# Two GNN layers on one core: x transposed in fp32 and halved on leaving PSUM, counts leaving PSUM two banks at a time, block copies shared by two engines, products two tiles late

## The chip, the core and the metric

One core of a Trainium2 chip runs the whole program. The metric is the device time of one execution in microseconds (us); lower is better. The engines are TensorE (PE in profiles), VectorE (DVE), ScalarE (ACT), GpSimd (POOL) and SyncE (SP), which issues the transfers.

## What is computed

3125 nodes with 256 features and 50,000 edges (src, dst), sorted by dst. Two graph layers, each followed by a residual sum and a layer norm:

```python
def _L0_gnn_ref(features, rows, cols, W0, b0, W1, b1):      # rows = src, cols = dst
    ...
    neigh = segment_sum(vals[:, None] * x[cols], rows)      # vals = 1 / degree
    cat = jnp.concatenate([x, neigh], axis=1)
    return relu(cat @ W.T + b)                              # twice, with W0 and W1

def _L1_gnn_ref(feat, W_self, W_neigh, src, dst):
    h_sparse = _maxk(feat @ W_neigh, 32)
    neigh = segment_sum(h_sparse[src], dst) / maximum(deg, 1)
    return feat @ W_self + neigh

x = _layernorm(x + _L0_gnn_ref(...))
x = _layernorm(x + _L1_gnn_ref(...))
```

## The kernel before

Sums over edges are made as products with a matrix of counts: C[s, d] is the number of edges between node s and node d. It is held in SBUF as 25 x 25 blocks of 125 x 125 counts in f16 (`ct`), and in HBM (`c_dram`) for the last layer. The program has four parts: the edges are sorted into windows (to about 58 us); the counts are built tile by tile ("the build", about 58 to 233 us, the part that the change touches); the first GNN's two sums and products; the second GNN.

**The build.** Tile t of 25 goes through these steps, each a program of its engine in a fixed written order, tied to the others by semaphores:

- VectorE writes one-hot rows for the edges of each window (`quick_hots(t, k)`, L790): 25 windows of a tile, in 3 sets. The rows of tile t+1 are written while tile t is counted; a set's buffer is free when its windows are counted.
- TensorE counts: `fill(t, f)` (L1336) multiplies the one-hot rows of 4 windows into one of 4 PSUM banks, 7 fills a tile.
- ScalarE copies each bank into a row of blocks in SBUF, `slab` (`quick_copy`, L1062), and SyncE stores the slab to `c_dram`.
- TensorE turns the slab's 25 blocks of the tile before in 4 groups (`transposes(t-1, par, g)`, L1359) into two banks, which alternate.
- VectorE copies each group from PSUM into `ct` (`tr_copy`, L796).

Beside this, the first product of x with W0 is made one tile of rows at a time. Values are carried as two f16 halves, a high and a low one, so that three f16 products stand for one fp32 product. GpSimd makes scale, high half and low half of x (`split_x`: L479, L480, L483), TensorE turns the four f16 quarters (`own_transposes`, L1373), ScalarE copies them to `x_t16` (`own_t`, L1073), TensorE multiplies (`own_product(t, 0)` and `(t, 1)`, L1367, three 512-column matmuls each), ScalarE copies the result to `own` (`own_copy`, L1080), and GpSimd splits its second half into `xs` (`split_a0`: L504, L506). The rows of x lie in `xs` as fp32 until then.

Ahead of the first products GpSimd also scales and splits the four weight matrices into halves (`split`, L479 to L483): 3 operations for each half of W0 and of W1, and 3 each for the two of the last layer. Its order is x tile 0, W0, x tile 1, W1, the last layer's two, and then, for each tile, the split of x and of the result. `own_copy(t)` waits for `split_a0(t-2)`, which frees its buffer.

The program's branch on the edges' total (`If`) holds the build's loop; the last tile's turns, and its product, stand behind the branch.

## Time and profile before

| | us |
|---|---|
| median of 3 runs (lowest, highest) | 754.15 (753.65, 754.87) |
| the profiled execution | 752.71 |
| its span, first to last instruction | 750.9 |
| TensorE busy in the span | 640.3 (85%) |
| VectorE busy | 542.4 (72%) |
| GpSimd busy | 370.4 (49%) |
| ScalarE busy | 318.6 (42%) |

The span is the profiled execution less what lies around the first and the last instruction (1.8 us). Shares of the whole span mix parts with different limits: what counts here is the build, in which VectorE has no idle time once it runs evenly, and the waits at its start.

### The profile page before, as it was taken

Reading aid. Unit: us, or ns where it says so; the run is one execution under the profiler, and the core shown is the slowest. Engines: PE = TensorE matmul, PEld = TensorE weight load, DVE = VectorE, ACT = ScalarE, POOL = GpSimd, SP = SyncE. Lnnn points to the kernel's source line nnn. Section 1 sums busy time; section 2 is a strip of 40 time slices with the busy share of each in tenths; the row PEclk is TensorE's granted clock in tenths of the full one; section 3 lists DMA queues with packets and bytes.
Section 4 is the critical chain, followed back from the end, with each engine's and each line's share of the span. In section 5 each row is a group of like instructions: output and inputs, shape, how many; then the busy total and the mean of one; then the engine's idle time right before and its main releaser. Section 6 shows DMA issues by size and latency. Waiting matters only on the chain.

```text
span 750.9 us, 11604 instructions
## 1 busy us (share of the span) xinstructions
PE 640.3 (85%) x4048; PEld 346.2 (46%) x4049; DVE 542.4 (72%) x1210; ACT 318.6 (42%) x672; POOL 370.4 (49%) x379
## 2 busy tenths in 40 slices
PE   2635387888778399999999999999999979999996
PEld 2524276666654144444444444444444434444443
DVE  6685489999981888888888546877877772844343
ACT  2122377777771567676776523333333320100000
POOL 2008999999984888888888222233233210000000
PEclk9755789999998699999999999999999999999999
DMA  9300346555553010111101046556555513320000
GB/s 229 48 20 22 99 128 213 149 150 149 147 157 96 9 42 29 41 33 38 41 29 42 23 137 180 157 171 180 168 159 178 173 57 103 111 82 21 28 21 28
DMA packets 39832, 72.99 MB, mean 97 GB/s; under 512 B 3609, under 2 KB 32496, under 8 KB 39770
## 3 DMA queue, kind: packets, MB, share of 16 engines
q1 hardware_dynamic: 39770, 72.20, 33.2%
q8 instruction: 35, 0.57, 0.3%
q14 instruction: 27, 0.22, 0.1%
HBM read 38.81 MB, written 33.38 MB: 96 GB/s over the span
## 4 chain that ended last, share of the span: by engine, by line
PE 53%; DVE 30%; POOL 5%; DMA 5%; issue 3%; ACT 2%; SPq 1%; DVEq 0%; POOLq 0%; ACTq 0%
PE bank L1461 26%; PE bank L1549 17%; DVE hots L790 12%; PE bank L1367 8%; DVE ct L796 5%; DMA xs<-in_x_dram 3%; DVE tree L872 2%; DVE tree L871 2%; POOL w_parts L483 1%; POOL w_scaled L479 1%; PE bank L1373 1%; DMA own_in<-own_dram 1%; POOL w_parts L480 1%; DVE xmax L633 1%; DMA bias_sb<-in_L_gnn_b_dram 1%
## 5 line engine op out<-in xcount | busy, mean ns | idle before, releaser
L1461 PE MATMUL bank<-xs,ct 125*128 125x512 f16 x625 | 147.2, 387 | 0.0
L1461 PE MATMUL bank<-a,ct 125*128 125x512 f16 x625 | 142.8, 379 | 0.0
L1549 PE MATMUL bank<-xs,ct 125*128 125x512 f16 x625 | 135.7, 379 | 0.0
L1062 ACT ACTIVATE slab<-bank 125x500 f16<-125x500 f32 (+1 forms) x175 | 92.5, 566 | 53.9 <-PE bank L1336 47.7
L790 DVE TENSOR_TENSOR hots<-iota,jobs 128x2048 f16<-128x2048 f16 (+1 forms) x75 | 107.4, 1434 | 2.7 <-issue 1.5
L1549 PEld LDWEIGHTS bank<-xs,ct 125*128 125x128 f16 x625 | 62.1, 99 | 72.3
L1461 PEld LDWEIGHTS bank<-xs,ct 125*128 125x128 f16 x625 | 61.9, 101 | 70.5 <-issue 4.9
L1461 PEld LDWEIGHTS bank<-a,ct 125*128 125x128 f16 x625 | 61.0, 99 | 68.2
L1161 ACT ACTIVATE a<-ct 125x1000 f16<-125x1000 f16 (+1 forms) x75 | 80.2, 1069 | 9.5 <-POOL tr_sb L548 8.6
L1359 PE MATMUL bank<-ident,slab 125*128 125x125 f16 x625 | 53.3, 224 | 30.8 <-DVE ct L796 25.9
L1367 PE MATMUL bank<-w_lay,tr_sb 128*128 128x512 f16 x300 | 73.0, 379 | 4.8 <-ACT tr_sb L1137 4.8
L562 POOL TENSOR_TENSOR part<-t,part 125x256 f16<-125x256 f32 x25 | 16.8, 672 | 117.1 <-ACT part L1201 117.1
L796 DVE COPY ct<-bank 125x882 f16<-125x882 f16 (+1 forms) x100 | 53.8, 556 | 25.2 <-PE bank L1359 25.2
L1336 PE MATMUL bank<-hots 128*128 128x125 f16 x625 | 54.3, 227 | 4.7 <-DVE hots L790 4.1
L887 DVE SCALAR_TENSOR_TENSOR t<-bank,rdeg,own_in 125x256 f32<-125x256 f32 x50 | 24.2, 484 | 46.9 <-PE bank L1461 42.3
L1359 PEld LDWEIGHTS bank<-ident,slab 125*128 125x128 f16 x625 | 39.2, 101 | 40.9 <-issue 22.9
L1223 ACT ACTIVATE sd<-mv,epsb 125x1 f32<-125x1 f32 x25 | 7.4, 294 | 113.9 <-DVE mv L992 113.9
L988 DVE SCALAR_TENSOR_TENSOR a<-bank,rdeg_dst,a 125x256 f32<-125x256 f32 x25 | 12.1, 482 | 56.5 <-PE bank L1549 56.4
L534 POOL TENSOR_TENSOR own_in<-own_in,bias_sb 125x256 f32<-125x256 f32 x50 | 39.3, 786 | 25.1 <-DMA own_in<-own_dram 25.1
L1336 PEld LDWEIGHTS bank<-hots 128*128 128x128 f16 x625 | 43.7, 103 | 15.1 <-DVE hots L790 4.5
L479 POOL TENSOR_TENSOR xscaled<-xs,scales 125x256 f32<-125x256 f32 x25 | 35.0, 1398 | 31.2 <-DVE scales L770 31.1
L1137 ACT ACTIVATE tr_sb<-bank 128x500 f16<-128x500 f32 x50 | 29.1, 582 | 47.2 <-PE bank L1373 47.2
(182 smaller groups left out, 1009.5 us busy)
## 6 DMA issues: line engine op xcount, KB each, us to landing
c_dram<-slab SPq DMA_DIRECT2D x25, 683.6 KB
ct<-c_dram SPq DMA_DIRECT2D x25, 683.6 KB
own_in<-own_dram SPq DMA_DIRECT2D x50, 125.0 KB
own_dram<-own SPq DMA_DIRECT2D x25, 125.0 KB
own_dram<-own_st SPq DMA_DIRECT2D x25, 125.0 KB
x_in<-in_x_dram SPq DMA_DIRECT2D x25, 125.0 KB
z_dram<-z_st SPq DMA_DIRECT2D x25, 125.0 KB
a<-z_dram SPq DMA_DIRECT2D x5, 625.0 KB
```

Source lines behind the costliest of these rows:

```text
L479: nc.gpsimd.tensor_tensor(scaled, given, by, ALU.mult).then_inc(pool_step, 1)
L534: nc.gpsimd.tensor_tensor(own_in[k % 2][:, :], own_in[k % 2][:, :], bias_sb[:, :], ALU.add).then_inc(own_biased, 1)
L790: v.tensor_tensor(hots[k][:, :, :, :].rearrange("p w g (a d) -> p (w g) a d", d=2), iota, job, ALU.is_equal).then_inc(win_hot, 1)
L796: v.tensor_copy(ct[:, TG0[g]:TG0[g] + TG[g], t, :], tr16[g % 2][0:P, 0:TG[g], 0:PC]).then_inc(tr_free, 1)
L1062: a.activation(slab3[t % 2][:, :, f * BW * QW:(f * BW + n) * QW].rearrange("p b (w d) -> p b w d", d=QW), bank[(FILLS * t + f) % 4][0:P, 0 ...
L1137: a.activation(tr_sb[i % 2][:, :, 0:P], tp[i % 2], ACT.Copy).then_inc(tp_copied, 1)
L1161: a.activation(unread[:, 0:(hi - lo) * P].rearrange("p (b s) -> p b s", s=P), ct[:, lo:hi, T, 0:P], ACT.Copy, accum_out=deg_part[:, T, k:k ...
L1336: last = mm(bank[n % 4][:, at:at + QKEY], hot[:, 0, :], hot[:, 1, 0:QKEY], start=True, stop=True, skip_group_check=True)
L1359: last = nc.tensor.transpose(tr16[g % 2][:, i, 0:P], slab[par][:, (TG0[g] + i) * P:(TG0[g] + i) * P + 128], ident16[:, 0:P])
L1367: last = mm(out, lhs(2 * pt + h), w[:, h, q, :], start=h == 0 and k == 0, stop=h == 1 and k == 2, skip_group_check=True)
L1461: ins = mm(agg[k % 3][0:lhs.shape[1], :], lhs, parts[l][:, t, :], start=t == 0, stop=t == NT - 1, skip_group_check=True)
L1549: ins = mm(out3[T % 8][0:lhs.shape[1], :], lhs, xs[:, b, :], start=b == 0, stop=b == NT - 1, skip_group_check=True)
```

## The change

- One-hot sets and fills become the same four groups, of 7, 6, 6 and 6 windows. A fill writes a pair of banks (two pairs in all), and one ScalarE copy empties a pair: 4 copies a tile instead of 7.
- The slab's blocks are turned in groups of 5, 8, 5 and 7. ScalarE copies groups 0 and 2 out of one bank, VectorE groups 1 and 3 out of the other.
- x is no longer split by GpSimd. TensorE turns its fp32 rows (two 128-column blocks), ScalarE writes the scaled high half (`own_t`), and VectorE the low half (`own_low`), both from PSUM. `own_product` waits for the low half.
- W0's high halves are written by ScalarE after tile 1, its low halves by VectorE (`w0_low`) at iteration 2.
- The products start in iteration 2 (tile of rows 0), iteration 3 has two (1 and 2), and from iteration 4 on each has one (t-1) as before.
- Some small work ahead of the build: two maxima of x instead of three and one over them, fewer steps for the scales, the clearing of two banks before the bounds instead of after them.

The core of the diff (the branch for other edge totals, semaphores and names of buffers are left out):

```diff
-SETS = [(0, 8), (8, 16), (16, 25)]
-BW = 4
-FILLS = 7
+SETS = [(0, 7), (7, 13), (13, 19), (19, 25)]
+FILLS = len(SETS)
 SHIFTS = [64, 32, 16, 8]
-XC = [0, 9, 17, 25]
+XC = [0, 13, 25]
+OWN = {2: [0], 3: [1, 2], **{t: [t - 1] for t in range(4, NT)}}
...
-TG = [7, 6, 6, 6]
-TG0 = [0, 7, 13, 19]
+TG = [5, 8, 5, 7]
+TG0 = [0, 5, 13, 18]
...
-            def split_x(t):
-                if t > 1:
-                    pool.wait_ge(own_tp, t - 1)
-                split(xparts[t % 2][:, 0:F], xparts[t % 2][:, F:2 * F], xscaled[:, :], xs32[:, t, :],
-                      scales[0:P, 0:1].broadcast_to([P, F]), x_split, t + 1)
...
-            split_x(0)
-            split_w(w_t[0], w0_parts, 3, w0_split, 1)
-            split_x(1)
             split_w(w_t[1], w_parts[0], 4, w_split, 1)
...
-            for t in range(2, NT):
-                split_x(t)
-                split_a0(t - 2)
-            split_a0(NT - 2)
-            split_a0(NT - 1)
+            for t in range(NT):
+                split_a0(t)
...
-            for c in range(3):
-                v.tensor_reduce(xmax[:, c:c + 1], xs32[:, XC[c]:XC[c + 1], :].rearrange("p t f -> p (t f)"), X, ALU.max,
+            for c in range(2):
+                v.tensor_reduce(stat[0:P, c:c + 1], xs32[:, XC[c]:XC[c + 1], :].rearrange("p t f -> p (t f)"), X, ALU.max,
...
+            def w0_low(h):
+
+                dve.wait_ge(w0_hi, h + 1)
+                lo = w0_parts[:, h, 1, :].rearrange("p (a f) -> p a f", a=2)
+                hi = w0_parts[:, h, 0, :].rearrange("p (a f) -> p a f", a=2)
+                v.scalar_tensor_tensor(lo, w_t[0][:, h::2, :], scales[:, 3:4], hi, ALU.mult, ALU.subtract).then_inc(w0_split, 1)
+
+            def own_low(t):
+
+                dve.wait_ge(own_tcopied, t + 1)
+                v.scalar_tensor_tensor(x_t16[:, 2:4, 0:P], xp, scales[:, 0:1], x_t16[:, 0:2, 0:P], ALU.mult, ALU.subtract
+                                       ).then_inc(own_tlo, 1)
...
-                    tr_copy(t - 1, 0)
-                    if t + 1 < NT:
+                    if t == 2:
+                        w0_low(0)
+                        w0_low(1)
+                    tr_copy(t - 1, 1)
+                    more = t + 1 < NT
+                    if more:
                         quick_hots(t + 1, 0)
-                    tr_copy(t - 1, 1)
-                    if t + 1 < NT:
+                    own = OWN.get(t, [])
+                    if more:
                         quick_hots(t + 1, 1)
-                    tr_copy(t - 1, 2)
+                    for o in own[:1]:
+                        own_low(o)
                     tr_copy(t - 1, 3)
-                    if t + 1 < NT:
+                    if more:
                         quick_hots(t + 1, 2)
-                for g in range(4):
+                        quick_hots(t + 1, 3)
+                    for o in own[1:]:
+                        own_low(o)
+                for g in (1, 3):
...
-                n = min(BW, NT - BW * f)
-                a.activation(slab3[t % 2][:, :, f * BW * QW:(f * BW + n) * QW].rearrange("p b (w d) -> p b w d", d=QW),
-                             bank[(FILLS * t + f) % 4][0:P, 0:n * QKEY].rearrange("p (w b d) -> p b w d", b=NT, d=QW),
+                lo, hi = SETS[f]
+                n = hi - lo
+                a.activation(slab3[t % 2][:, :, lo * QW:hi * QW].rearrange("p b (w d) -> p w b d", d=QW),
+                             pair[f % 2][0:P, 0:n, 0:QKEY].rearrange("p w (b d) -> p w b d", d=QW),
                              ACT.Copy).then_inc(slab_ready if f == FILLS - 1 else win_read, 1)
...
-                a.activation(x_t16[:, :, 0:P], tp[2], ACT.Copy).then_inc(own_tcopied, 1)
+                a.activation(x_t16[:, 0:2, 0:P], xp, ACT.Copy, scale=scales[:, 0:1]).then_inc(own_tcopied, 1)
...
+                for h in range(2):
+                    a.activation(w0_parts[:, h, 0, :].rearrange("p (a f) -> p a f", a=2), w_t[0][:, h::2, :], ACT.Copy,
+                                 scale=scales[:, 3:4]).then_inc(w0_hi, 1)
...
                     for f in range(FILLS):
                         quick_copy(t, f)
-                        if f == 1:
-                            own_t(t - 1)
-                    own_copy(t - 1, (t - 1) % 2, (t - 1) // 2)
+                        if f == 0:
+                            tr_copy(t - 1, 0)
+                        if f == 1 and own:
+                            own_t(own[0])
+                        if f == 2:
+                            tr_copy(t - 1, 2)
+                    if t == 1:
+                        ready_for_own()
+                    for i, o in enumerate(own):
+                        if i:
+                            own_t(o)
+                        own_copy(o, o % 2, o // 2)
+                for g in (0, 2):
+                    tr_copy(NT - 1, g)
...
-                k = 0 if f < 2 else 1 if f < 4 else 2
-                pe.wait_ge(win_hot, 3 * t + k + 1)
-                if n >= 4:
-                    t4, f4 = divmod(n - 4, FILLS)
-                    if f4 == FILLS - 1:
-                        pe.wait_ge(slab_ready, t4 + 1)
+                pe.wait_ge(win_hot, n + 1)
+                if n >= 2:
+                    t2, f2 = divmod(n - 2, FILLS)
+                    if f2 == FILLS - 1:
+                        pe.wait_ge(slab_ready, t2 + 1)
                     else:
-                        pe.wait_ge(win_read, (FILLS - 1) * t4 + f4 + 1)
-                for u in range(BW * f, min(BW * f + BW, NT)):
-                    hot, at = hots[k][:, u - SETS[k][0]], u % BW * QKEY
-                    last = mm(bank[n % 4][:, at:at + QKEY], hot[:, 0, :], hot[:, 1, 0:QKEY], start=True, stop=True,
+                        pe.wait_ge(win_read, (FILLS - 1) * t2 + f2 + 1)
+                for u in range(SETS[f][1] - SETS[f][0]):
+                    last = mm(pair[f % 2][:, u, 0:QKEY], hots[f][:, u, 0, :], hots[f][:, u, 1, 0:QKEY], start=True, stop=True,
                               skip_group_check=True)
...
-            def own_transposes(t, par):
-
-                pe.wait_ge(x_split, t + 1)
-                turn(tp[2], xparts[par], own_tp)
+            def own_transposes(t, rows_):
+
+                for h in range(2):
+                    last = nc.tensor.transpose(xp[:, h, :], rows_[:, h * 128:(h + 1) * 128], identx[:, :])
+                last.then_inc(own_tp, 1)
...
                 if h == 0:
-                    pe.wait_ge(own_tcopied, t + 1)
+                    pe.wait_ge(own_tlo, t + 1)
                     pe.wait_ge(own_copied, t + 1)
...
                 for t in range(1, NT):
                     par = (t - 1) % 2
+                    own = OWN.get(t, [])
                     fill(t, 0)
                     transposes(t - 1, par, 0)
+                    for o in own[:1]:
+                        own_transposes(o, xs32[:, o, :])
+                    transposes(t - 1, par, 1)
                     fill(t, 1)
-                    own_transposes(t - 1, par)
-                    transposes(t - 1, par, 1)
                     fill(t, 2)
+                    transposes(t - 1, par, 2)
+                    for o in own[:1]:
+                        own_product(o, 0)
+                    transposes(t - 1, par, 3)
                     fill(t, 3)
-                    transposes(t - 1, par, 2)
-                    own_product(t - 1, 0)
-                    fill(t, 4)
-                    fill(t, 5)
-                    transposes(t - 1, par, 3)
-                    own_product(t - 1, 1)
-                    fill(t, 6)
+                    for o in own[:1]:
+                        own_product(o, 1)
+                    for o in own[1:]:
+                        own_transposes(o, xs32[:, o, :])
+                        own_product(o, 0)
+                        own_product(o, 1)```

What this does to the order on the engines, in an iteration of the build's loop away from its ends.

TensorE before, iteration 4: `hots` rows are counts, `slab` rows turned blocks, `xparts` rows x turned in f16, `w_parts` rows the product's halves.

```order
L1336 MATMUL bank<-hots_63 128x125 x3
L1373 MATMUL bank<-ident_51,xparts_85 128x125 [waits x_split]
L1373 MATMUL bank<-ident_51,xparts_85 128x125 x3
L1359 MATMUL bank<-ident_51,slab_61 128x125 [waits tr_free,slab_ready]
L1359 MATMUL bank<-ident_51,slab_61 128x125 x5
L1336 MATMUL bank<-hots_64 128x125 [waits win_read,win_hot]
```

TensorE in the changed kernel, the same stretch and on to the product's second half (`xs` rows turn x in fp32):

```order
L1374 MATMUL pair<-hots_63 128x125 x6
L1397 MATMUL bank<-ident_51,slab_61 128x125 [waits tr_free0,slab_ready]
L1397 MATMUL bank<-ident_51,slab_61 128x125 x4
L1417 MATMUL bank<-identx,xs 128x125 x2
L1397 MATMUL bank<-ident_51,slab_61 128x125 [waits tr_free1,slab_ready]
L1397 MATMUL bank<-ident_51,slab_61 128x125 x7
...
L1405 MATMUL bank<-w_parts,x_t_84 125x512 [waits w0_split,own_copied,own_tlo]
L1405 MATMUL bank<-w_parts,x_t_84 125x512 x2
L1397 MATMUL bank<-ident_51,slab_61 128x125 [waits tr_free1,slab_ready]
L1397 MATMUL bank<-ident_51,slab_61 128x125 x6
L1374 MATMUL pair<-hots_66 128x125 [waits win_read,win_hot]
```

The turn of x no longer waits for GpSimd, and the product's first half, which waits for the low half (`own_tlo`), stands ahead of the last group of turned blocks.

VectorE before, one iteration:

```order
L796 COPY ct<-bank 125x7x126 [waits tr_done]
L790 TENSOR_TENSOR hots_63<-iota_67,jobs 128x2048 [waits win_done]
L796 COPY ct<-bank 125x6x126 [waits tr_done]
L790 TENSOR_TENSOR hots_64<-iota_67,jobs 128x2048 [waits win_done]
L796 COPY ct<-bank 125x6x126 [waits tr_done] x2
L790 TENSOR_TENSOR hots_65<-iota_67,jobs 128x2304 [waits win_done]
```

VectorE in the changed kernel, one iteration:

```order
L797 COPY ct<-bank 125x8x126 [waits tr_done]
L791 TENSOR_TENSOR hots_63<-iota_68,jobs 128x1792 [waits win_done]
L791 TENSOR_TENSOR hots_64<-iota_68,jobs 128x1536 [waits win_done]
L779 SCALAR_TENSOR_TENSOR x_t_84<-bank,scales,x_t_84 128x2x125 [waits own_tcopied]
L797 COPY ct<-bank 125x7x126 [waits tr_done]
L791 TENSOR_TENSOR hots_65<-iota_68,jobs 128x1536 [waits win_done]
L791 TENSOR_TENSOR hots_66<-iota_68,jobs 128x1536 [waits win_done]
```

Two of four block copies are gone, a fourth one-hot operation and the low half of x have come; the low half stands directly ahead of the copy of the last group of turned blocks.

## Rows read from the trace of the kernel before

**Rows 1.** The page: busy time by engine in the span.

```profile
PE 640.3 (85%) x4048; PEld 346.2 (46%) x4049; DVE 542.4 (72%) x1210; ACT 318.6 (42%) x672; POOL 370.4 (49%) x379
```

**Rows 2.** Windows of the even build: stretch, busy (instructions), PEclk, DMA share, GB/s.

```profile
102.30:216.39 114.09, 90.37 (x1143) 71.71 (x1141) 114.09 (x134) 85.67 (x171) 109.86 (x96) 1.00 0.55 163
```

**Rows 3.** Chain of waits in an even iteration: start, us, what.

```profile
144.42 1.62 DVE hots L790
...
148.30 0.53 DVE ct L796
148.83 1.13 DVE hots L790
```

**Rows 4.** Groups by form, even build: count, busy, mean ns, idle before.

```profile
L1062 ACT ACTIVATE slab<-bank 125x500 f16<-125x500 f32 x114 | 64.7, 607 | 21.4 <-PE bank L1336 21.2
L1080 ACT ACTIVATE own<-bank,unscale 125x512 f32<-125x512 f32 x19 | 12.8, 675 | 0.0
L1062 ACT ACTIVATE slab<-bank 125x125 f16<-125x125 f32 x19 | 6.0, 317 | 6.4 <-PE bank L1336 6.4
```

**Rows 5.** Timeline of TensorE, even iteration: start, us, instruction [idle before].

```profile
148.97 0.49 PE L1359 MATMUL bank<-ident,slab 125*128 125x125 f16 x6 [0.56 <-DVE ct L796]
149.30 0.81 PE L1367 MATMUL bank<-w_parts,x_t 128*125 128x512 f16 x3
149.95 0.60 PE L1336 MATMUL bank<-hots 128*128 128x125 f16 x8
```

**Rows 6.** Timeline of GpSimd, the same stretch.

```profile
142.89 1.32 POOL L504 CAST xs<-own 125x256 f16<-125x256 f32 x1
144.29 0.67 POOL L506 TENSOR_TENSOR xs<-own,xs 125x256 f16<-125x256 f32 x1
```

**Rows 7.** Timeline of VectorE, to the fourth iteration: start, us, instruction [idle before].

```profile
60.06 1.35 DVE L790 TENSOR_TENSOR hots<-iota,jobs 128x2304 f16<-128x2304 f16 x1
...
73.57 0.55 DVE L796 COPY ct<-bank 125x756 f16<-125x756 f16 x1 [7.06 <-PE bank L1359]
...
94.05 0.55 DVE L796 COPY ct<-bank 125x756 f16<-125x756 f16 x1 [9.81 <-PE bank L1359]
...
100.18 0.60 DVE L796 COPY ct<-bank 125x882 f16<-125x882 f16 x1
```

**Rows 8.** Timeline of GpSimd: its first operation, weights beside VectorE and in quiet.

```profile
58.94 0.61 POOL L479 TENSOR_TENSOR xscaled<-xs,scales 125x256 f32<-125x256 f32 x1 [31.08 <-DVE scales L770]
...
76.98 1.90 POOL L479 TENSOR_TENSOR w_scaled<-w_t,scales 128x512 f32<-128x512 f32 x1
...
87.45 1.04 POOL L479 TENSOR_TENSOR w_scaled<-wn_nat,scales 128x512 f32<-128x512 f32 x1
```

**Rows 9.** The page: a VectorE operation that reads PSUM in fp32.

```profile
L887 DVE SCALAR_TENSOR_TENSOR t<-bank,rdeg,own_in 125x256 f32<-125x256 f32 x50 | 24.2, 484 | 46.9 <-PE bank L1461 42.3
```

**Rows 10.** Timeline of TensorE: fp32 turns, and a product at half clock.

```profile
30.09 1.15 PE L1240 MATMUL bank<-identf,w_nat 128*128 128x128 f32 x8 [0.96 <-ACT w_t L1025]
...
95.28 1.49 PE L1367 MATMUL bank<-w_parts,x_t 128*125 128x512 f16 x3
```

**Rows 11.** Windows of TensorE: stretch, busy, PEclk, DMA share, GB/s.

```profile
94.00:96.00 2.00, 2.00 (x17) 0.50 0.00 0
222.00:226.00 4.00, 1.99 (x26) 1.00 0.43 129
226.00:230.00 4.00, 1.54 (x22) 0.69 0.50 140
```

**Rows 12.** Timeline of TensorE at the end of the build.

```profile
223.44 0.22 PE L1336 MATMUL bank<-hots 128*128 128x125 f16 x1
225.66 0.55 PE L1359 MATMUL bank<-ident,slab 125*128 125x125 f16 x7 [2.01 <-issue]
...
230.46 2.77 PE L1367 MATMUL bank<-w_parts,x_t 128*125 128x512 f16 x6
```

**Rows 13.** Timeline of VectorE, the last copy of the build.

```profile
230.71 0.55 DVE L796 COPY ct<-bank 125x756 f16<-125x756 f16 x1 [2.61 <-PE bank L1359]
```

More of the change, by code:

```diff
@@ L543, in sum_tree @@
                 nc.gpsimd.tensor_tensor(tree[:, :], tree[:, :], quint[4], ALU.add).then_inc(tree_ready, 1)
-            pool.wait_ge(tr_free, 4 * NT + 2)
+            for done in tr_free:
+                pool.wait_ge(done, 2 * NT + 1)
             sum_tree(0)
@@ L816, in _ @@
             with dve.If(total > E - 1):
-                for k in range(3):
+                for k in range(FILLS):
                     quick_hots(0, k)
@@ L844, in _ @@
                 scales_out()
-                with dve.Fori(0, NW) as w:
-                    general_hots(w)
-            dve.wait_ge(tr_free, 4 * NT + 2)
+                for u in range(WT):
+                    general_hots(u)
+                for h in range(2):
+                    w0_low(h)
+                with dve.Fori(1, NT) as t:
+                    for u in range(WT):
+                        general_hots(t * WT + u)
+                        if u == 1:
+                            v.tensor_copy(xstage[:, :], xs32[:, ds(t - 1, 1), :].rearrange("p o f -> p (o f)")).then_inc(own_staged, 1)
+                        if u == 2:
+                            own_low(t - 1)
+            own_low(NT - 1)
+            for free in tr_free:
+                dve.wait_ge(free, 2 * NT + 1)
             dve.wait_ge(slab_stored[0], BOTH * 13)
@@ L1001, in _ @@
             act.sem_inc(win_free, 2)
-            act.sem_inc(tr_free, 2)
+            for free in tr_free:
+                act.sem_inc(free, 1)
             act.wait_ge(firsts_b, 2)
@@ L1163, in _ @@
             act.wait_ge(tr_zeroed, 2)
-            act.wait_ge(tr_free, 4 * NT + 2)
+            for free in tr_free:
+                act.wait_ge(free, 2 * NT + 1)
             for k in range(len(DG)):
```

98 lines of the change are left out of this document (53 added, 45 removed).

## Prediction

> **What bounds the kernel now.** The page comes first: TensorE is busy 85% of the span, VectorE 72% [rows 1], but the change is in the build alone, so I read that part by windows and by its chain of waits. From 102.30 us, where the build runs evenly, to 216.39 us pass 19 iterations of 6.005 us, and VectorE is busy for all of it; TensorE has 90.4 of 114.1 us, ScalarE 85.7, GpSimd 109.9 [rows 2]. The chain there is VectorE alone: one-hots, the first of 1.62 and the last of 1.13 us, and block copies, such as one of 0.53 us [rows 3]. Both one-hots have 2048 elements, and the first is 0.49 us longer. GpSimd's L506 is running when it starts (144.29 us for 0.67 us), and L504 takes 1.32 us, most of it beside a one-hot [rows 6]. So an iteration loses half a us where the two share something.
>
> Ahead of the even part VectorE waits 7.06 and 9.81 us for turned blocks [rows 7]. TensorE stands there behind products and turns of x whose halves GpSimd has yet to write. That is the second thing the change touches.
>
> **What the change does, step by step.** I count from start to start of operations, and call the sets H0 to H3, the groups of turned blocks T0 to T3, the counts F0 to F3, the turn of x X, the product's halves P0 and P1, VectorE's copies R1 and R3, and the low half of x L.
>
> *VectorE's own work.* The quiet one-hot takes 1.13 us for 2048 elements, the copy 0.53 for 882 [rows 3]: 0.515 ns an element and 0.075 us fixed, if both run alike. So H0 (1792) is 1.00 us and H1 to H3 (1536) 0.865 each: 3.6 us. The copy of 882 elements takes 0.53 us [rows 3]; R1 has 1008 (0.6) and R3 882 (0.53). L reads 250 fp32 elements a partition from PSUM; the nearest row, of that kind with 256, takes 0.484 us [rows 9]. The sum, with L overlapped as usual (0.4), is 5.1 us against 6.0. By this alone an iteration would win 0.9 us.
>
> *But VectorE does not run alone.* The order is L, R3 on VectorE and P0, T3 on TensorE: P0 waits for L, T3 stands behind P0, and R3 waits for T3. Between L and R3 VectorE has nothing to do. TensorE's three 512-column matmuls take 0.65 us (149.30 to 149.95), six turned blocks 0.33 us (148.97 to 149.30), 0.055 each, and the last of a group ends 0.16 us later [rows 5]. From L's start to R3's: 0.48 (L) + 0.14 (to TensorE, as from the copy's end at 148.83 to the blocks' start at 148.97 [rows 3, 5]) + 0.65 (P0) + 0.39 (T3, 7 blocks) + 0.20 (end and signal) = 1.86 us. The circle through VectorE is then 1.86 + 0.53 (R3) + 1.73 (H2, H3) + 0.60 (R1) + 1.87 (H0, H1) = 6.6 us.
>
> *A second circle, through TensorE, is as long.* R1 waits for T1, which is late: 0.62 (L) + 0.65 (P0) + 0.39 (T3) + 0.33 (F3) + 0.65 (P1) + 0.39 (F0) + 0.28 (T0) + 0.28 (X) + 0.44 (T1) + 0.20 + 0.60 (R1) + 1.87 (H0, H1) = 6.7 us. X is two fp32 turns: eight took 1.15 us at full clock, 0.14 each [rows 10]. ScalarE's circle is shorter. Its copy costs 0.317 us for 125 columns and 0.607 us for 500 [rows 4], 0.77 ns a column; back to back four copies of a pair (0.80 and three of 0.70), two of 630 elements (0.59 each), the high half (0.3) and the result (0.57) give 5.0 us. The new write pattern (runs of five elements) has no row: bounds are nothing and a fifth more, 0.6 us, still under the circle.
>
> *The collision stays.* L504 starts when the result is copied, by this schedule 3.8 us after L's start, while H3 runs (3.3 to 4.2); it ends behind it, and L506 runs from about 4.5 to 5.2, over H0's start at 4.8. H0 loses 0.45 us, as the first one-hot does now. Both circles hold H0, so the period is 7.1 us. Without the collision it would be 6.6. **I take 7.1**, for the row shows this very pair [rows 3, 6]. On what the two share, the Trainium skill (SBUF — State Buffer, Who interferes with whom) says that VectorE and GpSimd have one pair of ports, held by one of them for a whole instruction. The trace agrees, with 1.62 against 1.13 us; were it not so here, the period would be 6.6 us.
>
> *The start.* Before, the fourth iteration's first copy starts at 100.18 us [rows 7]. Now GpSimd no longer stands between TensorE and x or W0. VectorE ended the last one-hot of tile 1 at 60.06 + 1.35 = 61.4 us [rows 7]; that set is smaller now, which gives 61.0, and I count the dropped small steps at nothing. Iteration 1 costs 4.7 us of VectorE's own, about 1 for waiting on T3 at half clock, and 1 for collisions with the weights' split, which goes on: to 67.7. The two `w0_low` (512 fp32 elements from two SBUF sources) add 1.2 and up to 0.9 of waiting: to 69.8. R1, H0, H1 and 0.8 of collisions: L at 73.1. From there 7.1 us to the next L, and 2.2 more since TensorE has been idle and begins at half clock, where three matmuls read 1.49 instead of 0.81 us [rows 5, 10] and the granted clock 0.50 [rows 11]: L of iteration 3 at 82.4. That iteration has a second product: X, L, 1.3 us for both halves, all ahead of F0: 7.1 + 3.4 = 10.5 us to the next L, at 92.9. Its iteration began 2.9 us earlier (R1, H0 with its collision, H1), at 90.0. **The start wins 10.2 us** (bounds 5 and 15: a little more half clock, or none and no collisions).
>
> GpSimd must have split the result of tile 0 when ScalarE wants to write that of tile 2, at about 88 us. It has 12 weight operations, of 1.04 us in quiet and 1.90 beside VectorE, from about 58.9 us on [rows 8]: with each at 1.9 they are done at 82, and `split_a0(0)` at 84. Covered.
>
> *The even part.* 20 iterations from there: 20 x (7.1 - 6.005) = +21.9 us. The last one has no one-hots; from its first copy to the end of the last count are 2.8 us, before 3.4: -0.6.
>
> *The tail.* Before, the last count ends at 223.66 us, the last turns follow a 2.01 us gap behind the branch, and the product starts at 230.46 us [rows 12], a quarter us before VectorE's last copy starts at 230.71 [rows 13]. Now that product waits for the last L, which stands behind that copy and behind VectorE's own branch. If leaving it costs VectorE what it costs TensorE, 2 us, L starts 2.6 us after the copy does and the product ends 3 us later than before: +3 (bounds 0.5 and 3.5).
>
> The sum: -10.2 + 21.9 - 0.6 + 3.0 = +14.1 us on the profiled execution's 752.7, that is 766.8; the median of the runs shown is 1.4 us above that execution: 768.
>
> **The rivals.**
>
> *No collision* (0.20). L504 and L506 fall between one-hots: the period is 6.65, the even part +12.9, the sum +5.1, 759 us. Against it: they follow the result's copy at a fixed distance. For it: 0.3 us of shift would free H0.
>
> *VectorE's own work sets the pace* (0.12, the faster side). TensorE has P0 and T3 done before VectorE wants R3, because L's data are there early or the last blocks wait elsewhere. Then the period is 5.1 plus a collision, 5.6: 20 x -0.4 = -8.1, the sum -10.2 - 8.1 - 0.6 + 3 = -16, 738 us. It decides from a period of 6.4 on, where 20 x 0.39 equals what start and tail leave over. For it: VectorE is now the pace alone [rows 2, 3]. Against it: the written order of L, P0, T3, R3.
>
> *The sum is nothing* (0.05): a period of 6.4, or of 6.6 with the whole 15 us won at the start and a short tail: 754 us.
>
> *TensorE's clock falls in every iteration* (0.08). It would be idle some 2 us between T2 and P0 in each. The rows: with 1.99 us busy of 4 the granted clock was 1.00, with 1.54 in the next four it fell, mean 0.69 [rows 11]; the new iteration has about 4.7 us busy of 7.1, well over half. If it fell, P0, T3, F3 and P1 would take twice their 2.0 us: 9.1 a period, +40 us, 808 us. The Trainium skill (TensorE: Matmul & The Clock Gate, HAM oscillation — how this bites in real kernels) tells of kernels whose every burst starts at the lower clock, since the wait ahead of it was long; by it this is the case to fear.
>
> **How the numbers follow.** The forecast has 0.55. A difference within 0.2% (1.5 us) can't be told from none. Slower: 0.55 + 0.20 + 0.08 = 0.83; same 0.05; faster 0.12. The range: the low end is a start of 15 won, a period of 6.6, a tail of 0.5: -15 + 12 - 0.6 + 0.5 = -3, 751 us; the high end a start of 5, 7.4 and 3.5: -5 + 28 - 0.6 + 3.5 = +26, 780 us. That leaves out the two ends' rivals, 0.2 together.
>
> **What would show it.** Right: VectorE idle some 1.4 us ahead of the second block copy in each iteration, released by turned blocks; TensorE's idle time ahead of the product's first half, released by VectorE's L; one-hots of 1792 elements lasting about 1.5 us where 1.07 is their quiet length; an even period of 7.1 us; no waits of 7 and 10 us in the start. Wrong: VectorE without idle time and a period under 6.4; a PEclk under 1 in the even part; ScalarE ahead of TensorE's counts as the releaser, its copies far over 0.9 us; GpSimd's weights not done at 88 us.

## The result, and the profile after

The changed kernel takes 770.07 us (median of 4 runs, 769.11 to 772.88) against 754.28 (753.65 to 754.87) for the kernel before: a ratio of 1.0208, 95% interval 1.0184 to 1.0233. The profiled execution took 769.11 us. The page after, span and busy time by engine, then groups of instructions as in [rows 1] and [rows 9]:

```profile
span 766.4 us, 11302 instructions
PE 648.2 (85%) x3998; PEld 347.2 (45%) x3999; DVE 530.2 (69%) x1203; ACT 355.4 (46%) x649; POOL 261.4 (34%) x300
...
L1405 PE MATMUL bank<-w_parts,x_t 128*125 128x512 f16 x150 | 44.1, 407 | 45.7 <-DVE x_t L779 45.7
```

GpSimd lost 109 us of work and VectorE 12, and the kernel is longer. The products wait 45.7 us in all for VectorE's low half L (L779). That wait is new.

The window of the even build after, which answers to [rows 2] (busy time of TensorE, its weight loads, VectorE, ScalarE and GpSimd, in this order):

```profile
97.28:228.46 131.18, 94.64 (x1106) 72.11 (x1104) 101.36 (x133) 112.35 (x153) 24.86 (x39) 1.00 0.48 141
```

Nineteen iterations take 131.2 us, 6.905 each, where they took 6.005. VectorE was busy for all of the time and now has 30 us idle. TensorE idles more than before, and its granted clock stays at 1.00.

VectorE's timeline in one even iteration after (R1, H0 and H1, L, R3, H2 and H3); it answers to [rows 3]:

```profile
138.70 0.68 DVE L797 COPY ct<-bank 125x1008 f16<-125x1008 f16 x1 [0.23 <-PE bank L1397]
139.30 2.00 DVE L791 TENSOR_TENSOR hots<-iota,jobs 128x1792 f16<-128x1792 f16 x2
141.23 0.47 DVE L779 SCALAR_TENSOR_TENSOR x_t<-bank,scales,x_t 128x250 f16<-128x250 f32 x1
143.03 0.62 DVE L797 COPY ct<-bank 125x882 f16<-125x882 f16 x1 [1.34 <-PE bank L1397]
143.57 1.82 DVE L791 TENSOR_TENSOR hots<-iota,jobs 128x1536 f16<-128x1536 f16 x2
```

There are two waits for turned blocks: 1.34 us behind L, and 0.23 us ahead of R1. The second says that the circle through TensorE is the longer one, if only just. The chain of waits after, from L to the next L:

```profile
141.30 0.40 DVE x_t L779
...
141.75 0.86 PE bank L1405 x3
142.61 0.39 PE bank L1397 x7
143.00 0.35 PE pair L1374 x6
...
143.37 1.06 ACT slab L1087
...
144.47 0.45 PE bank L1397 x5
144.92 0.22 PE bank L1417 x2
145.14 0.45 PE bank L1397 x8
...
145.62 0.68 DVE ct L797
146.30 1.91 DVE hots L791 x2
```

Read it down: L, P0, T3, the last fill F3, **ScalarE's copy of F3**, T0, X, T1, R1, H0 and H1. T0 turns the slab that this copy completes, so it waits for the copy, which takes longer than the work TensorE has meanwhile (P1 and F0). The groups of ScalarE's pair copy and of the one-hots over the even window after:

```profile
L1087 ACT ACTIVATE slab<-pair 125x750 f16<-125x750 f32 x57 | 60.9, 1069 | 18.8 <-PE pair L1374 18.8
...
L791 DVE TENSOR_TENSOR hots<-iota,jobs 128x1792 f16<-128x1792 f16 x19 | 21.4, 1125 | 0.0
```

GpSimd's timeline beside the iteration above; compare [rows 6]:

```profile
145.00 0.64 POOL L502 CAST xs<-own 125x256 f16<-125x256 f32 x1 [5.51 <-ACT own L1105]
145.72 0.67 POOL L504 TENSOR_TENSOR xs<-own,xs 125x256 f16<-125x256 f32 x1
```

The subtraction ends at 146.39, and the next H0 starts at 146.22: they overlap by 0.17 us. Before, the one-hot that met it started at 144.34 and the subtraction ended at 144.96, an overlap of 0.62 us:

```profile
144.34 1.70 DVE L790 TENSOR_TENSOR hots<-iota,jobs 128x2048 f16<-128x2048 f16 x1
```

Where the 15.5 us of span went, by marks in both traces (the predicted values beside them):

| stretch | before | after | difference | predicted |
|---|---|---|---|---|
| to the fourth iteration's first block copy | 100.18 | 90.42 | -9.8 | -10.2 |
| from there to the end of the last count | 123.48 | 142.39 | +18.9 | +21.3 |
| from there to the first sum with the counts | 9.36 | 12.45 | +3.1 | +3.0 |
| from there to the end | 517.9 | 521.1 | +3.2 | 0 |

The marks of the tail, on TensorE's timeline after (last count; first of the last turned blocks; last product; first sum), and the first sum before:

```profile
232.32 0.49 PE L1374 MATMUL pair<-hots 128*128 128x125 f16 x6
...
235.65 0.53 PE L1397 MATMUL bank<-ident,slab 125*128 125x125 f16 x5 [2.18 <-issue]
...
242.64 2.82 PE L1405 MATMUL bank<-w_parts,x_t 128*125 128x512 f16 x6 [3.44 <-DVE x_t L779]
245.26 10.51 PE L1510 MATMUL pair<-xs,ct 125*128 125x512 f16 x46
```

```profile
233.02 3.20 PE L1461 MATMUL bank<-xs,ct 125*128 125x512 f16 x11
```

### The profile page after: what moved, and what is told of

Its sections match the earlier page's. It is cut to its first block, busy times and chain, and to the rows that moved or that the text cites. A ratio compares the mean times of both kernels' runs of the same rounds, so it can differ in the third digit from the quotient of the medians.

```text
span 766.4 us, 11302 instructions
## 1 busy us (share of the span) xinstructions
PE 648.2 (85%) x3998; PEld 347.2 (45%) x3999; DVE 530.2 (69%) x1203; ACT 355.4 (46%) x649; POOL 261.4 (34%) x300
## 4 chain that ended last, share of the span: by engine, by line
PE 60%; DVE 24%; DMA 5%; ACT 5%; issue 4%; POOL 1%; SPq 0%; DVEq 0%; ACTq 0%; POOLq 0%
PE pair L1510 25%; PE bank L1600 9%; PE pair L1600 8%; DVE hots L791 8%; PE bank L1405 7%; PE bank L1397 4%; PE pair L1405 3%; ACT slab L1087 3%; DMA xs<-in_x_dram 3%; DVE ct L797 2%; DVE tree L895 2%; DVE tree L894 2%; DVE x_t L779 1%; PE pair L1374 1%; PE bank L1411 1%
## 5 line engine op out<-in xcount | busy, mean ns | idle before, releaser
L1510 PE MATMUL pair<-xs,ct 125*128 125x512 f16 x625 | 146.5, 386 | 0.0
L1510 PE MATMUL pair<-a,ct 125*128 125x512 f16 x625 | 142.8, 379 | 0.0
L1087 ACT ACTIVATE slab<-pair 125x875 f16<-125x875 f32 (+1 forms) x100 | 109.5, 1099 | 39.6 <-PE pair L1374 39.6
L791 DVE TENSOR_TENSOR hots<-iota,jobs 128x1792 f16<-128x1792 f16 (+1 forms) x100 | 99.6, 1035 | 1.5 <-issue 1.5
L1510 PEld LDWEIGHTS pair<-xs,ct 125*128 125x128 f16 x625 | 61.9, 101 | 70.3 <-issue 4.6
L1510 PEld LDWEIGHTS pair<-a,ct 125*128 125x128 f16 x625 | 61.0, 99 | 68.1
L1200 ACT ACTIVATE a<-ct 125x1000 f16<-125x1000 f16 (+1 forms) x75 | 80.2, 1069 | 9.6 <-POOL tr_sb L541 8.7
L1405 PE MATMUL bank<-w_parts,x_t 128*125 128x512 f16 x150 | 44.1, 407 | 45.7 <-DVE x_t L779 45.7
L1600 PE MATMUL bank<-xs,ct 125*128 125x512 f16 (+1 forms) x325 | 71.5, 379 | 0.0
L1600 PE MATMUL pair<-xs,ct 125*128 125x512 f16 x300 | 68.1, 386 | 0.0
L797 DVE COPY ct<-bank 125x1008 f16<-125x1008 f16 (+1 forms) x50 | 32.5, 650 | 45.6 <-PE bank L1397 45.6
L1374 PE MATMUL pair<-hots 128*128 128x125 f16 x625 | 53.0, 225 | 10.3 <-ACT slab L1087 5.9
L502 POOL CAST xs<-own 125x256 f16<-125x256 f32 x25 | 15.0, 600 | 136.9 <-ACT own L1105 136.9
L1397 PE MATMUL bank<-ident,slab 125*128 125x125 f16 x625 | 53.1, 225 | 6.8 <-issue 2.2
L1397 PEld LDWEIGHTS bank<-ident,slab 125*128 125x128 f16 x625 | 41.4, 101 | 19.7 <-issue 9.0
L1374 PEld LDWEIGHTS pair<-hots 128*128 128x128 f16 x625 | 41.2, 101 | 18.7 <-issue 9.5
```

What stands on the lines that cost most here:

```text
L791: v.tensor_tensor(hots[k][:, :, :, :].rearrange("p w g (a d) -> p (w g) a d", d=2), iota, job, ALU.is_equal).then_inc(win_hot, 1)
L797: v.tensor_copy(ct[:, TG0[g]:TG0[g] + TG[g], t, :], tr16[1][0:P, 0:TG[g], 0:PC]).then_inc(tr_free[1], 1)
L1087: a.activation(slab3[t % 2][:, :, lo * QW:hi * QW].rearrange("p b (w d) -> p w b d", d=QW), pair[f % 2][0:P, 0:n, 0:QKEY].rearrange("p w ( ...
L1200: a.activation(unread[:, 0:(hi - lo) * P].rearrange("p (b s) -> p b s", s=P), ct[:, lo:hi, T, 0:P], ACT.Copy, accum_out=deg_part[:, T, k:k ...
L1374: last = mm(pair[f % 2][:, u, 0:QKEY], hots[f][:, u, 0, :], hots[f][:, u, 1, 0:QKEY], start=True, stop=True, skip_group_check=True)
L1397: last = nc.tensor.transpose(tr16[g % 2][:, i, 0:P], slab[par][:, (TG0[g] + i) * P:(TG0[g] + i) * P + 128], ident16[:, 0:P])
```

## The experiments

Ratios are to the kernel before on the same chip (medians there 755.26, 755.66 and 755.35 us), with 95% intervals. The changed kernel has 1.0208. A period is read from R1 to R1, around 140 us.

### 1. T3 ahead of P0

```diff
+                    transposes(t - 1, par, 3)
                     for o in own[:1]:
                         own_product(o, 0)
-                    transposes(t - 1, par, 3)
                     fill(t, 3)
```

> One exchange of the changed kernel's order on TensorE: the last group of turned blocks (T3) stands ahead of the product's first half (P0), so VectorE's second block copy no longer waits for x's low half L through P0. My theory: the even period of 6.90 us is the circle L, P0, T3, F3, ScalarE's copy of F3, T0, X, T1, R1, H0, H1; T3's 0.39 us leave it, so the period is 6.5 us, and VectorE's 1.34 us wait ahead of R3 is gone or far shorter; about 762 us. Rival 1: ScalarE's seven operations with their slow copies set the pace: the period stays at 6.9 us, 770 us. Rival 2: only the circle over R3 binds (VectorE's own 5.1 us plus its wait): the period falls by the whole wait to 5.6 us, 744 us.

758.36 us, 1.0048 (1.0031 to 1.0065). VectorE's timeline:

```profile
142.00 0.68 DVE L797 COPY ct<-bank 125x1008 f16<-125x1008 f16 x1 [1.29 <-PE bank L1397]
...
144.86 0.60 DVE L797 COPY ct<-bank 125x882 f16<-125x882 f16 x1
...
148.47 0.68 DVE L797 COPY ct<-bank 125x1008 f16<-125x1008 f16 x1 [1.27 <-PE bank L1397]
```

R3's wait is gone, and the period is 6.47. The idle time did not vanish. It stands ahead of R1 now: the circle through TensorE is left alone, shorter by the T3 (0.39 us) that has gone from between P0 and F3. So the order P0, T3 is one of the causes, and there is another.

### 2. T3 and F3 ahead of both halves of the product

```diff
+                    transposes(t - 1, par, 3)
+                    fill(t, 3)
                     for o in own[:1]:
                         own_product(o, 0)
-                    transposes(t - 1, par, 3)
-                    fill(t, 3)
```

> Both product halves stand behind the last count (order T2, T3, F3, P0, P1). My theory: L's way back to VectorE is then L 0.44, P0 and P1 1.30, F0 0.39, T0 0.28, X 0.22, T1 0.63, R1 0.60, H0 and H1 1.91, that is 5.8 us; ScalarE's own work is 5.7 us, so the period is 5.8 to 6.1 us, 20 periods win 16 to 22 us: 748 to 754 us. Rival 1 (ScalarE sets the pace now, 5.91 us busy of 6.90 with waits that belong to it): the period stays above 6.6 us, over 764 us. Rival 2 (TensorE's clock falls in the gaps): no change here, since it was 1.00 throughout.

747.78 us, 0.9886 (0.9859 to 0.9913), faster than the kernel before. The period is 5.87. VectorE still waits 0.67 us ahead of R1. ScalarE has no idle time left (the fourth busy time, 111.34 of 111.34 us):

```profile
96.86:208.20 111.34, 94.23 (x1104) 72.92 (x1102) 98.72 (x133) 111.34 (x153) 20.17 (x38) 1.00 0.56 166
```

The order of three calls is worth 22 us between the medians, 24 by the ratios. Both circles ran through P0 and what stands behind it.

### 3. ScalarE writes runs of 30 elements, not of 5

```diff
-    ... .rearrange("p b (w d) -> p w b d", d=QW),
-    ... .rearrange("p w (b d) -> p w b d", d=QW),
+    ... .rearrange("p b (w d) -> p b w d", d=QW),
+    ... .rearrange("p w (b d) -> p b w d", d=QW),
```

> ScalarE's copy of a count pair writes as the kernel before did, in runs of a block's 30 or 35 columns, and reads PSUM across windows; all else is the changed kernel. Theory: the write pattern (runs of five f16 elements) is what makes the copy take 1.07 us for 750 columns where 0.77 ns a column and 0.2 us fixed would give 0.80. Then copies take 0.80 us, F3's copy falls out of the circle by 0.25 us, the path over P1 and F0 takes its place at 6.7 us, and GpSimd's L504 runs over H0 again, so H0 and H1 together take 2.0 to 2.3 instead of 1.99 us: period 6.7 to 6.85, 766 to 769 us. Rival 1: reading two banks at once is the cost: copies stay at 1.07 us and the time at 770. Rival 2: ScalarE sets the pace: four copies 0.25 us shorter give a period of 5.9 us, 750 us.

770.53 us, 1.0224 (1.0187 to 1.0262). The edit changes both sides of the copy: it writes longer runs, and it reads PSUM across windows, 5 columns at a time. The copy is shorter, 837 ns (group over 100 to 200 us):

```profile
L1087 ACT ACTIVATE slab<-pair 125x750 f16<-125x750 f32 x43 | 36.0, 837 | 25.6 <-PE pair L1374 25.6
```

But the period stays 6.90, where 6.7 to 6.85 was expected. VectorE's timeline, and GpSimd's, show why:

```profile
146.31 0.68 DVE L797 COPY ct<-bank 125x1008 f16<-125x1008 f16 x1
146.91 2.22 DVE L791 TENSOR_TENSOR hots<-iota,jobs 128x1792 f16<-128x1792 f16 x2
...
150.87 0.62 DVE L797 COPY ct<-bank 125x882 f16<-125x882 f16 x1 [1.34 <-PE bank L1397]
```

```profile
145.74 0.82 POOL L502 CAST xs<-own 125x256 f16<-125x256 f32 x1 [5.33 <-ACT own L1105]
146.65 0.67 POOL L504 TENSOR_TENSOR xs<-own,xs 125x256 f16<-125x256 f32 x1
```

R1 no longer waits. The circle through R3 binds now, and it holds the collision that was predicted: the subtraction runs to 147.32 over H0, and H0 with H1 takes 2.22 us. What the shorter copy gave, the collision took.

### 4. The same, with GpSimd let go by L

```diff
                 pool.wait_ge(own_copied, t + 2)
+                pool.wait_ge(own_tlo, min(t + 2, NT))
```

> The write-pattern kernel, in which H0 and H1 took 2.23 us, with one wait more: GpSimd splits the result of tile t only after VectorE's low half of tile t+1, that is in VectorE's idle 1.34 us ahead of R3. Theory: the 0.3 us over the quiet 1.91 us are GpSimd's subtraction holding what both need; moved into the idle time it costs nothing, H0 and H1 take 1.9 us, and the period falls from 6.90 to 6.6 us (the circles over R3, 6.6, and over T1, 6.7): 763 to 766 us. Rival: the one-hots are longer for another reason (ScalarE's or the transfers' traffic): 2.2 us, 6.9 us and 770 us stay.

766.81 us, 1.0143 (1.0096 to 1.0189). VectorE's and GpSimd's timelines:

```profile
139.64 0.69 DVE L798 COPY ct<-bank 125x1008 f16<-125x1008 f16 x1
140.24 1.95 DVE L792 TENSOR_TENSOR hots<-iota,jobs 128x1792 f16<-128x1792 f16 x2
...
146.27 0.68 DVE L798 COPY ct<-bank 125x1008 f16<-125x1008 f16 x1
```

```profile
142.71 0.40 POOL L503 CAST xs<-own 125x256 f16<-125x256 f32 x1 [5.49 <-DVE x_t L780]
143.19 0.67 POOL L505 TENSOR_TENSOR xs<-own,xs 125x256 f16<-125x256 f32 x1
```

GpSimd now works while VectorE idles behind L. The period is 6.63: 0.27 us less, and nothing but GpSimd's place was changed against experiment 3. That isolates the collision.

### 5. The last product's halves inside the branch

```diff
-                for g in (1, 3):
-                    tr_copy(NT - 1, g)
+                tr_copy(NT - 1, 1)
+                own_low(NT - 1)
+                tr_copy(NT - 1, 3)
...
-            own_low(NT - 1)
```

On ScalarE the high half moves likewise, between its two last copies.

> Only the end is changed: ScalarE's high half and VectorE's low half of the last tile stand inside the branch, between the last block copies, instead of behind it. Theory: the tail's extra 3.1 us are the two engines' ways out of the branch (2.16 and 2.25 us without work), which the last product waits for. Then the last product starts right behind the last turned blocks, 2.5 to 3.2 us earlier: 767 us. Rival: the last product would start late anyway (its weights or TensorE's own gap of 2.2 us): under 1 us, 769 to 770 us.

766.64 us, 1.0135 (1.0101 to 1.0169). TensorE's timeline at the end of the build:

```profile
237.47 0.50 PE L1376 MATMUL pair<-hots 128*128 128x125 f16 x6
...
243.37 2.77 PE L1407 MATMUL bank<-w_parts,x_t 128*125 128x512 f16 x6
245.93 4.42 PE L1512 MATMUL pair<-xs,ct 125*128 125x512 f16 x19
```

The product no longer waits for L, and from the last count's end (237.97) to the first sum are 7.96 us instead of 12.45. So the whole growth of the tail (3.1 us), and 1.4 us more, came from the place of the two halves behind the branch. The ratio fell by 0.0073, 5.5 us. This kernel equals the changed one up to the tail, yet its profiled execution reached the fourth iteration's first copy at 94.24 us, 3.8 later, 1.4 of it ahead of the build's first block copy; more on that under 8.

### 6. 2, 3 and 5 together

> Three edits together: products behind the last count, ScalarE's old write pattern, the last tile's halves inside the branch. With products last the period was 5.87 us and ScalarE had no idle time; its four copies lose 0.2 us each, so it falls to about 5.0 us of work and the circle of L over P0, P1, F0, T0, X, T1, R1, H0, H1 takes over at 5.75 us, plus up to 0.3 us if GpSimd meets H0. Period 5.75 to 6.0 us, so little from the write pattern (0 to 2 us in all), 3 us from the tail: 742 to 746 us. Rival: ScalarE was the only bound, the period falls to VectorE's own 5.2 us and the time to 733 us.

741.25 us, 0.9822 (0.9784 to 0.9859). The period is 5.87 once more, and R1's wait is still 0.67 us, though ScalarE's copies are short here and it has idle time again. So ScalarE was full in experiment 2 but did not set the pace, and the write pattern is worth nothing there. What is left is the circle that starts at L: L comes late in VectorE's order, and the product behind it holds F0, T0 and T1.

### 7. L ahead of H1, then GpSimd between the one-hots

```diff
                     own = OWN.get(t, [])
+                    for o in own[:1]:
+                        own_low(o)
                     if more:
                         quick_hots(t + 1, 1)
-                    for o in own[:1]:
-                        own_low(o)
```

On ScalarE `own_t` moves ahead of `tr_copy(t - 1, 0)` to be in time.

> The combined kernel, and x's halves earlier in the iteration: ScalarE writes the high half before block copy 0, VectorE the low half before H1. H1 (0.9 us) leaves L's circle, which then has 4.9 us; what is left is VectorE's own work, 5.2 us, plus what GpSimd's two operations take of it (0.1 to 0.5). Period 5.3 to 5.7 us: 6 to 10 us under the combined kernel, 734 to 740 us. Rival: L only waits for ScalarE where it now stands (the high half is not ready), and the period stays at 5.8 us or over.

730.45 us, 0.968 (0.9643 to 0.9717), a little better than expected. VectorE has no idle time left and the period is 5.46. Its timeline still shows a collision in H0, with GpSimd's subtraction (143.32 to 143.99). The cast ran beside H3, which took its quiet length:

```profile
143.50 1.44 DVE L791 TENSOR_TENSOR hots<-iota,jobs 128x1792 f16<-128x1792 f16 x1
```

The last edit lets GpSimd go only once the first one-hot of the next set is written:

```diff
                 pool.wait_ge(own_copied, t + 2)
+                pool.wait_ge(win_hot, min(FILLS * (t + 3) + 1, FILLS * NT))
```

> The kernel with the low half before H1 (period 5.46 us, VectorE without idle time, H0 1.36 us where 0.98 is quiet), with one wait more: GpSimd starts to split a result only when H0 of the next iteration is written, so its cast meets L and its subtraction R3, both of which read PSUM. Theory: the 0.4 us come back, less what the subtraction (0.67 us) reaches over R3 (0.52 us): period 5.1 to 5.25 us, 20 periods win 4 to 7 us: 724 to 727 us. Rival: another circle (ScalarE 5.1 us of work, or L over P0, P1, F0, T0, X, T1, R1, H0 at 4.9) is as long as 5.4 us: no gain, 730 us.

726.08 us, 0.9605 (0.9587 to 0.9623). VectorE's and GpSimd's timelines:

```profile
144.24 1.07 DVE L792 TENSOR_TENSOR hots<-iota,jobs 128x1792 f16<-128x1792 f16 x1
145.24 0.47 DVE L780 SCALAR_TENSOR_TENSOR x_t<-bank,scales,x_t 128x250 f16<-128x250 f32 x1
```

```profile
145.45 0.40 POOL L503 CAST xs<-own 125x256 f16<-125x256 f32 x1 [3.46 <-DVE hots L792]
145.93 1.26 POOL L505 TENSOR_TENSOR xs<-own,xs 125x256 f16<-125x256 f32 x1
```

The period is 5.19 (143.65 to 148.84), close to the 5.1 of VectorE's own work. H0 has its quiet length. The cast starts beside L and is not held up; its end reaches over H1's start, which costs H1 0.09 us (1.03 for 0.94). The subtraction starts beside H1 and takes 1.26 us, which nobody waits for.

### 8. What sets the start

The question was whether the first iterations are slow by GpSimd's weight splits beside the one-hots, or by TensorE at half clock. First the splits were put off (W1's and the last layer's wait for W0's low halves), in the changed kernel:

```diff
+            pool.wait_ge(w0_split, 2)
             split_w(w_t[1], w_parts[0], 4, w_split, 1)
```

> The changed kernel with one edit in its start: GpSimd begins to split W1 and the last layer's weights only when VectorE has written W0's low halves. Theory: from 58.9 to 70.8 us VectorE runs beside GpSimd's splits; four one-hots take 6.2 us where 3.6 would do and the two w0_low 2.9 us where 1.2 would: 4.3 us. They are won there, and half is lost again as the splits then meet iterations 2 and 3, or ScalarE waits for GpSimd's first result: the fourth iteration's first copy at 86.5 to 88.5 us instead of 90.4, 766 to 768 us. Rival: the start is bound by TensorE at half clock, not by VectorE: no change, 770 us.

767.25 us, 1.0167 (1.0123 to 1.021). The time lies where it was expected, but its interval overlaps that of the changed kernel, and the start, where the gain was to come from, has none. The profiled span is 2.5 us shorter than the changed kernel's, and more than that, 3.1 us, lies behind the first sum, where the two kernels are the same. Rows of VectorE's timeline:

```profile
64.94 1.41 DVE L775 SCALAR_TENSOR_TENSOR w_parts<-w_t,scales,w_parts 128x512 f16<-128x512 f32 x2
66.27 0.68 DVE L798 COPY ct<-bank 125x1008 f16<-125x1008 f16 x1
66.86 3.27 DVE L792 TENSOR_TENSOR hots<-iota,jobs 128x1792 f16<-128x1792 f16 x2
...
91.34 0.68 DVE L798 COPY ct<-bank 125x1008 f16<-125x1008 f16 x1 [4.42 <-PE bank L1398]
```

Iteration 2 starts at 66.27 instead of 70.83, but the fourth at 91.34 instead of 90.42. The splits meet the one-hots of iterations 2 and 3 instead (3.27 us for a pair that takes 1.95 in quiet), and TensorE falls to a granted clock of 0.50 twice. To tell these two apart, 26 matmuls of 125 columns whose result nobody uses were added ahead of P0 in iterations 2 and 3; they only occupy TensorE:

```diff
                     transposes(t - 1, par, 2)
+                    if t in (2, 3):
+                        pe.wait_ge(own_copied, own[0] + 1)
+                        for _ in range(26):
+                            mm(bank[6][0:P, 0:P], ident16[:, 0:P], ident16[:, 0:P], ...)
```

> The kernel with GpSimd's weights later, and 26 matmuls of 125 columns without use ahead of the product's first half in iterations 2 and 3, where TensorE waited 3.0 and 3.3 us and then ran at half clock (three matmuls in 1.54 us instead of 0.86). Theory: the 4.1 us that this kernel had won by 66.3 us were lost to half clock: with the clock kept up, VectorE's waits of 2.37 us ahead of R3 become 1.34, the second product's six matmuls 1.5 instead of 2.8 us, and the fourth iteration's first copy stands at 87 to 88.5 us instead of 91.3: 763 to 765 us. Rival: GpSimd's splits, now beside iterations 2 and 3, are what took the 4 us: no change with the clock, 91 us, 767.

768.25 us, 1.0158 (1.0131 to 1.0184). Windows of the same stretch with and without them:

```profile
70.00:74.00 4.00, 2.55 (x26) 1.00 0.00 0
```

```profile
70.00:74.00 4.00, 3.42 (x18) 0.50 0.00 0
```

The clock was held in iteration 2, and the first wait for turned blocks fell from 2.37 to 1.34 us. Counted from the build's first block copy, R1 of iteration 3 comes after 15.7 us instead of 16.8, and that of iteration 4 after 30.5 instead of 31.2; the changed kernel takes 29.7. So half clock was worth about 1 us in iteration 2. Iteration 3 is not free of it: the granted clock was 0.86 from 78 us and 0.71 from 82 to 90, and the product's first half took 1.49 us. That iteration took 14.8 us where the changed kernel takes 10.0. Of the difference, 2.3 us are its longer one-hots (6.04 us for 3.77), beside the splits, and 2.6 us its longer waits for turned blocks (6.89 us for 4.26), at half clock. So the collisions had moved and still cost something, and about as much was half clock; what the later splits would give at full clock throughout was not run.

> The first kernel of this call with the same 26 matmuls in iterations 2 and 3. If half clock costs the start something there, 1 to 3 us are won over it; if GpSimd's splits beside VectorE set the start's length, nothing.

This puts the same matmuls into the kernel of experiment 7's last edit: 724.58 us, 0.9576 (0.955 to 0.9603), not to be told from 726.08. The fourth iteration's first copy stands at 88.63 (88.12 without): no gain. This does not decide between the two, for the clock was not held: the matmuls ran from 67.94 to 69.62 us, TensorE then idled 3.11 us, and the granted clock from 74 to 78 us was 0.50 with and without them. What the kernel without them does show is that half clock costs this order little in iteration 2: VectorE does not wait there for turned blocks.

One more comparison bears on the clock. From the build's first block copy to the fourth iteration's first, the changed kernel took 29.7 us and the kernel of experiment 5, the same up to there, 32.1. There the granted clock was 0.50 from 78 to 82 us and 0.60 from 86 to 90, where the changed kernel had 0.90 and 1.00, and R1 and R3 of iteration 3 waited 1.0 us longer each (1.80 for 0.76, 2.37 for 1.34). So when TensorE falls to 1.2 GHz in the start differed between these two executions, and was worth up to 2.4 us.

## Why the prediction was right

It said 768 us, between 751 and 780; 770.07 was measured. The mechanism was there, but that the total came so near is luck in part, as errors of opposite sign met in it.

**What bounds it: right.** The blocking was as it was told. L starts, P0 waits for it, T3 stands behind P0, R3 waits for T3; VectorE idles 1.34 us there (about 1.4 was predicted). The circle through VectorE, with no collision, was put at 6.6 us; experiment 4 measured it alone, 6.63.

**The second circle: its longest term was the wrong one.** The prediction filled the time between F3 and T0 with TensorE's own P1 and F0, 1.04 us. On TensorE's timeline P1 starts, behind F3, at 143.16, and T0 at 144.47: 1.31 us, of which the copy sets the end. The prediction had sized that copy (0.70 us for the pair of 6 windows when back to back, a fifth more for the new write pattern as a bound) and compared it only with ScalarE's own circle, "still under the circle". The copy took 1.07 us, against 0.84 in the old pattern (experiment 3, where R1 no longer waits). TensorE's row of P1:

```profile
143.16 0.81 PE L1405 MATMUL bank<-w_parts,x_t 128*125 128x512 f16 x3
```

The other terms came out within 0.1 us, 0.11 less in all, so the circle is 6.86 quiet and 6.90 with what is left of the collision.

**The collision: right as a mechanism, mis-sized here.** 0.45 us was counted, about 0.04 was there: H0 and H1 take 1.99 to 2.00 us in a row where they take 1.95 in quiet. The late copy of F3 holds R1, and so H0, back by 0.23 us, nearly clear of GpSimd's subtraction; the rival "no collision" had named 0.3 us as what would free H0. In experiment 3 the hold is gone and the collision back, 0.28 us. The two errors, +0.2 and -0.4, left 6.90 where 7.1 was said, -4 us over 20 iterations. So the rival "no collision" had its premise nearly met, and its 6.65 us failed by the copy alone. The predicted 1.5 us for a one-hot of 1792 elements was 1.13. On what is shared, the Trainium skill (SBUF — State Buffer, Who interferes with whom) says that an operation of VectorE with two SBUF inputs contends with GpSimd's reads, and that one with at most one SBUF input, outside VectorE's 2-port modes, does not. The trace agrees with both: H0 takes 1.44 us beside GpSimd and 1.07 without, and the cast takes its 0.40 us beside L, which reads one operand from PSUM. The prediction's "for a whole instruction" stands in the Trainium skill under those 2-port modes, and it gives operations of the one-hots' kind (two tensors) none; that H0 loses nearly all that is left of the subtraction agrees with it all the same.

**The last iteration: wrong, +0.9 where -0.6 was said.** From its first copy, at 228.48, the last count's end is 4.33 us away, not 2.8. Without one-hots VectorE is early, but the high half is not. VectorE's timeline after:

```profile
230.70 0.48 DVE L779 SCALAR_TENSOR_TENSOR x_t<-bank,scales,x_t 128x250 f16<-128x250 f32 x1 [1.54 <-ACT x_t L1098]
```

L waits 1.54 us for ScalarE, and P0, T3 and F3 stand behind L. This makes the 2.4 us between +18.9 and +21.3: -4.0 by the period, +1.5 by this.

**The start: the sum right, its parts less so.** L was told for 73.1, 82.4 and 92.9 us and came at 74.50, 82.91 and 92.89; GpSimd's weights were done at 76.7 (82 was the bound). That the collisions with the splits weigh is shown (experiment 8: the two `w0_low` 1.41 us without, 2.97 with them, where 1.2 and up to 0.9 more was said), that half clock does too (2.4 us between two executions). How the 10 us divide between them was not settled.

**The tail: right**, +3.1 for +3.0, with 2.25 us of idle time on VectorE and 2.16 on ScalarE behind the branch where 2 was assumed; experiment 5 shows the cause by removing it.

**TensorE's clock: the rival fell.** With gaps of 1.5 us in 6.9, it stayed at 1.00 for 131 us. What the Trainium skill (TensorE: Matmul & The Clock Gate, HAM oscillation — how this bites in real kernels) tells of, kernels in which every burst starts at the lower clock behind a long wait, did not happen in the even part. In the start the first product did begin so: TensorE idled 7.92 us ahead of the first product at 75.02, three matmuls then took 1.54 us, and the granted clock was 0.50 from 74 to 78 us.

**Not foreseen:** 3.2 us behind the build. The last layer's sums took 144.2 us with a granted clock of 0.98, and 142.9 with 1.00 before; and in the first layer, a product of six matmuls at 277.97 us took 2.58 us where one at 265.01 had taken 1.49. These are the same matmuls in number and shape. No experiment changes this stretch, and from the first sum to the end their eleven profiled executions took 517.5 to 520.5 us, the changed kernel 521.1 and the kernel before 517.9. So executions with the same work there differ by as much as was to be explained, and no cause in the change is shown.

## What to carry to other kernels

Where engines work in fixed orders and wait for each other, add up the closed circles, from an operation to its next turn; the longest one is the period, and busy time does not show it. On each circle put the longest of the parallel branches: between two steps of one engine, another's copy may be longer than what stands there. An operation whose data come late belongs behind all that others wait for: three calls in another order made 2% slower into 1% faster, and x's two halves, each moved ahead on its engine, gave another 1.4%.

## What the runs showed of the hardware

- ScalarE's copy of 750 fp32 columns from PSUM to f16 in SBUF took 1.07 us when it wrote runs of 5 elements, and 0.84 us when it wrote runs of 30 and read PSUM in runs of 5; for 875 columns 1.20 and 0.92 to 0.93 us.
- A GpSimd operation that is running when a one-hot starts costs it what is left of its own time, less 0.12 to 0.13 us, not a share: the one-hot was longer by 0.04, 0.28, 0.37 and 0.49 us where the subtraction had 0.17, 0.41, 0.49 and 0.62 us left (the changed kernel, experiments 3 and 7, the kernel before).
- Behind the branch each engine stood idle: 2.18 us on TensorE, 2.16 on ScalarE and 2.25 on VectorE in the changed kernel, TensorE's and VectorE's one after the other, as the last turned blocks lie between them. It is no fixed price: in the experiments TensorE's was 1.58 to 3.00 us and ScalarE's 1.86 to 3.75. The kernel before also has 2.21 us of it inside its last group of turned blocks (to 229.96), where no branch ends, so the branch as its cause was not isolated.
